# Channel mixing of the last layer moved from in front of the key scans to between and behind them

## What is computed

```python
x = x + _L3_attn_ref(xn, ...) + _L3_ffn_ref(xn, L3_ffn_W_r, L3_ffn_W_k, L3_ffn_W_v, L3_ffn_mu_r, L3_ffn_mu_k)

# attention: dx is a convolution over three tokens, less x
t5 = jnp.tanh((x + dx * maa_x) @ maa_w1).reshape(B, T, 5, 32)
m = jnp.einsum('btfc,fcd->fbtd', t5, maa_w2)
xw = x + dx * (maa_w + m[0])                     # also xk, xv, xr, xg
w_log = -jnp.exp(time_decay + jnp.tanh(xw @ decay_w1) @ decay_w2)
S = jnp.exp(wt)[..., None] * S + kt[..., None] * vt[..., None, :]     # forwards, and likewise backwards
yn = ((yg - mu) / jnp.sqrt(var + eps)).reshape(B, T, D) * ln_w + ln_b
return yn * g @ Wo                               # y is also gated by sigmoid(dx @ gate_w + gate_b)

# channel mixing
xr = mu_r * x + (1.0 - mu_r) * x_prev
xk = mu_k * x + (1.0 - mu_k) * x_prev
out = sigmoid(xr @ W_r.T) * (square(relu(xk @ W_k.T)) @ W_v.T)
```

## Time and profile before

| | |
|---|---|
| median of 3 runs | 2244.57 us |
| the profiled execution's own time | 2241.96 us |
| its span | 2240.1 us |
| last layer behind its layernorm | from about 1940 us to the end |
| TensorE matmul busy, whole span | 1997.6 us (89%) |
| VectorE busy, whole span | 1578.4 us (70%) |

### The profile page before, as it was taken

One profiled execution on the slowest core, in us unless ns is written; L12 is line 12 of the kernel. 1 busy time (PEld: TensorE's weight loads), 2 busy tenths in 40 slices (PEclk: granted clock), 3 DMA queues, 4 the chain that ended last, 5 costly groups with the idle time before them and its releaser, 6 DMA issues. The chain is left out here.

```text
span 2240.1 us, 56828 instructions
## 1 busy us (share of the span) xinstructions
PE 1997.6 (89%) x22888; PEld 1359.7 (61%) x22888; DVE 1578.4 (70%) x4071; ACT 1300.6 (58%) x2606; POOL 978.3 (44%) x1206
## 2 busy tenths in 40 slices
PE   4669998998999999999999797789999998688886
PEld 2548887996888887888888675533333343333322
DVE  6666664675666677767666645489898993689996
ACT  3337775555777777777777533147776777444323
POOL 2027776664667844566443224011111210058763
PEclk9779999999999999999999889679999999799998
DMA  7221111314011200000000017211111110000000
GB/s 186 97 78 37 39 38 48 100 30 159 21 38 20 39 7 2 21 2 21 2 2 3 1 53 233 63 23 39 39 39 39 40 41 4 27 0 1 10 5 24
DMA packets 77797, 93.46 MB, mean 42 GB/s; under 512 B 10017, under 2 KB 56114, under 8 KB 76002
## 3 DMA queue, kind: packets, MB, share of 16 engines
q1 hardware_dynamic: 64050, 76.54, 11.4%
q0 software_dynamic: 13488, 13.28, 3.0%
HBM read 53.87 MB, written 35.53 MB: 40 GB/s over the span
## 5 line engine op out<-in xcount | busy, mean ns | idle before, releaser
L1181 DVE TENSOR_REDUCE a_parts<-a_S 128x1 f32<-128x512 f32 (+1 forms) x576 | 362.8, 682 | 30.5 <-PE a_S L1065 24.3
L1152 ACT ACTIVATE WA<-a_E 128x1024 f32<-128x1024 f32 (+1 forms) x320 | 282.9, 939 | 119.0 <-PE a_E L1093 60.8
L478 POOL TENSOR_SCALAR WA<-WA,a1b_rinv 128x1024 f32<-128x1024 f32 (+3 forms) x192 | 142.0, 757 | 181.4 <-DVE a1b_rinv L817 181.2
L1057 PE MATMUL a_S<-a_KS,a_QS 54*128 54x512 bf16 (+3 forms) x768 | 190.1, 348 | 30.8 <-DVE a_parts L1181 18.8
L478 POOL TENSOR_SCALAR XR<-XR,a1b_rinv 128x768 f32<-128x768 f32 (+3 forms) x192 | 141.2, 749 | 118.4 <-DVE a1b_rinv L817 117.7
L633 PE MATMUL a1b_O<-a1b_PT,WA 128*64 128x128 f32 x3072 | 189.0, 276 | 0.0
L633 PEld LDWEIGHTS a1b_O<-a1b_PT,WA 128*64 128x64 f32 x3072 | 165.8, 137 | 6.5
L1057 PEld LDWEIGHTS a_S<-a_KS,a_QS 54*128 54x128 bf16 x768 | 58.8, 95 | 173.6 <-DVE a_parts L1181 136.2
L598 PE MATMUL a1b_B<-a1b_Kf,a1b_Qf 64*128 64x512 f32 (+2 forms) x768 | 155.1, 478 | 8.5 <-issue 4.6
L993 POOL CAST a_mrow<-WA 32x128 bf16<-32x128 f32 x16 | 4.5, 280 | 355.2 <-DVE WA L1194 355.2
L1105 PE MATMUL a_O<-WA,V 128*9 128x512 f32 (+3 forms) x1536 | 154.5, 489 | 0.1
(11 more groups left out here) (551 smaller groups left out, 5786.5 us busy)
## 6 DMA issues: line engine op xcount, KB each, us to landing
WA<-in_w SPq DMA_DIRECT2D x7, 1024.0 KB, 9.5
a_QS<-qstack SPq DMA_DIRECT2D x32, 216.0 KB
a_KS<-kstack SPq DMA_DIRECT2D x32, 216.0 KB
a1b_tb<-tab SPq DMA_DIRECT2D x12, 512.0 KB
qstack<-f_parts SPq DMA_DIRECT2D x24, 256.0 KB
kstack<-f_parts SPq DMA_DIRECT2D x24, 256.0 KB
f_slots<-f1r_zrows SPq DMA_DIRECT2D x9, 516.0 KB
f1t_xs<-f_slots SPq DMA_DIRECT2D x9, 516.0 KB, 7.3
```

What stands on the lines that cost most here:

```text
L478: pool.tensor_scalar(v, v, rinv[:, e, u, part:part + 1], 1.0, ALU.mult, ALU.mult).then_inc(n_sb, 1)
L1057: ins = pe.matmul(pS[(at + half) % SB][:, lo:lo + n], QS[s][ROW[half], pair, i * P:(i + 1) * P], KS[s][ROW[half], pair, block * P:block * ...
L1152: act.activation(PT[q % NP][:, :, 0:w], pE[q % 2][:, :, 0:w], ACT.Exp).then_inc(e_sb, 1)
L1181: dve.tensor_reduce(peak, pS[at % SB][:, :].rearrange("p (c k) -> p c k", c=n), AX.X, ALU.max)\
```

## The change

No chunk of the channel mixing lies in front of the first scan any more. Six lie between the scans: chunk 0 in steps 4 to 6 of batch 1, chunk 1 in the same steps of batch 2, and chunks 2 to 5 in batch 3, one for each two steps. Chunks 6 and 7 lie behind. The interpolation is gone: GpSimd makes four scaled weight matrices once, at the end of batch 0 (`weights`), and the products c_k and c_r are two accumulated matmuls each, on the tokens and on the tokens one earlier. The middle chunks' products c_k, c_r, c_v, c_t go through the ring of the two pC banks; ScalarE's part of them is `middle`, VectorE's parts are `weighed_mid` and `collect_mid`.

In front of the first scan t5b, d1 and d2 of batch 0 go to pY ("FRONT") and pass the ring by; m_g of batch 0 and its mixing move behind the first scan; the products k come after `values(0)`; and GpSimd no longer waits for the interpolation. In step 7 the output product of the batch before now lies between r and g. At the end the normalisation of batch 3 is done in halves by two VectorE operations each, `scaled` and `final`, without ScalarE's affine step, and one-element activations on ScalarE load the tables of tanh and, at the end, of the logarithm early. ScalarE calls `middle(c)` behind `deviation` or `decay` in batches 1 and 2, and between the steps of the normalisation in batch 3.

```diff
...
-    EARLY = 3
-    SLOT = tuple(c % 3 for c in range(2 * B))
-    LAST_IN = (None, None, None) + tuple(range(2 * B - 3))
-    mdx, mxr, mxk = (ph.sb(n, [P, 3, CH]) for n in ("mdx", "mxr", "mxk"))
-    mkr = [Sf[0][:, 0:CH], Sf[0][:, CH:T], Sf[1][:, 0:CH]]
-    mdelta = [Sr[0][:, 0:CH], Sr[0][:, CH:T], Sr[1][:, 0:CH]]
-    msig = [Sf[1][:, CH:T], Sr[1][:, CH:T], Sr[2][:, 0:CH]]
-    low = [t[:, 0:CH] for t in (*pV, pY)]
-    high = [t[:, CH:T] for t in (*pV, pY)]
-    l_dx, l_mixed, l_rk, l_relu, l_k2, l_sig, l_v, l_delta, l_tr, l_x = (
-        ph.sem(n) for n in ("ldx", "lmixed", "lrk", "lrelu", "lk2", "lsig", "lv", "ldelta", "ltr", "lx"))
+    MID = (0, 1, 2, 3, 4, 5)
+    SLOT = {6: 0, 7: 1}
+    TURN = {c: n for n, c in enumerate(SLOT)}
+    ck, cr, cw = (ph.sb(n, [P, T]) for n in ("ck", "cr", "cw"))
+    mkr = [Sf[0][:, 0:CH], Sf[0][:, CH:T]]
+    mdelta = [Sr[0][:, 0:CH], Sr[0][:, CH:T]]
+    msig = [Sr[1][:, 0:CH], Sr[1][:, CH:T]]
+    low = [t[:, 0:CH] for t in pV]
+    high = [t[:, CH:T] for t in pV]
+    FRONT = {("t5b", 0, 0): pY[:, CH:T], ("d1", 0, 0): pY[:, 0:CH], ("d2", 0, 0): pY[:, 0:CH], ("d2", 0, 1): pY[:, CH:T]}
+    sides = (slice(0, CH), slice(CH, T))
...
-    START = {0: NEXT[0], 1: NEXT[1], 2: NEXT[2], 3: NEXT[3][:1], 4: NEXT[4], 5: NEXT[3][1:], 6: NEXT[5][3:],
-             7: NEXT[5][2:3] + NEXT[6]}
+    STILL = {0: ((("r", 0),), (("r", 1),), (("m_g", 0), ("m_g", 1))), 2: ((("gate", 0),), (("gate", 1),)),
+             3: ((("g", 0),), (("g", 1),))}
+    START = (("t5a", 0),), (("t5a", 1),), (("t5b", 0),), (("m_w", 0), ("m_v", 0)), (("m_w", 1), ("m_v", 1)), (("d1", 0),), \
+        (("m_k", 0), ("m_r", 0)), (("d2", 0), ("d2", 1)), (("m_k", 1), ("m_r", 1)), (("k", 0),), (("k", 1),)
+    ONE = {4: (("c_k", 0), ("c_r", 0)), 5: (("c_v", 0),), 6: (("c_t", 0),)}
+    FOUR = {0: (("c_k", 2), ("c_r", 2)), 1: (("c_v", 2),), 2: (("c_t", 2), ("c_k", 3), ("c_r", 3)), 3: (("c_v", 3),),
+            4: (("c_t", 3), ("c_k", 4), ("c_r", 4)), 5: (("c_v", 4),), 6: (("c_t", 4), ("c_k", 5), ("c_r", 5)), 7: (("c_t", 5),)}
...
-        after = of(b + 1, NEXT[v]) if b + 1 < B else []
         front = of(b - 1, LAST.get(v, ())) if b else of(0, STILL.get(v, ()))
-        return after + front if v == 7 else front + after
-
-    ring = [key for v in range(HK) for group in of(0, START[v]) for key in group]
+        if b + 1 == B:
+            return ([(("c_v", 5, 0),)] if v == 7 else []) + front + [((kind, c, 0),) for kind, c in FOUR[v]]
+        after = of(b + 1, NEXT[v])
+        mixing = [((kind, b - 1, 0),) for kind, c in ONE.get(v, ())] if b else []
+        return (after[:2] + front + after[2:] if v == 7 else front + after) + mixing
...
+        key = (kind, b, h)
+        return FRONT[key] if key in FRONT else pC[turn_of[key] % 2]
...
+            def weights():
+                pool.tensor_scalar(wk1[:, :], mw_k, mu_k, None, ALU.mult)
+                pool.tensor_scalar(wr1[:, :], mw_r, mu_r, None, ALU.mult).then_inc(l_wd, 1)
+                pool.wait_ge(l_wd, 1)
+                pool.tensor_tensor(wk0[:, :], mw_k, wk1[:, :], ALU.subtract)
+                pool.tensor_tensor(wr0[:, :], mw_r, wr1[:, :], ALU.subtract).then_inc(l_w, 1)
...
-            pool.wait_ge(l_mixed, EARLY)
...
-                n = place[kind, b, h]
+                if (kind, b, h) in FRONT:
+                    if kind == "d2":
+                        pe.wait_ge(emptied["t5b"], 1)
+                    return
+                n = turn_of[kind, b, h]
...
+                elif kind == "c_k":
+                    pe.wait_ge(l_w, 1)
+                    pe.matmul(out[:, :], wk1[:, :], tokens(b, 1), start=True, stop=False)
+                    ins = pe.matmul(out[:, :], wk0[:, :], tokens(b, 0), start=False, stop=True)
+                elif kind == "c_r":
+                    pe.matmul(out[:, :], wr1[:, :], tokens(b, 1), start=True, stop=False)
+                    ins = pe.matmul(out[:, :], wr0[:, :], tokens(b, 0), start=False, stop=True)
+                elif kind == "c_v":
+                    pe.wait_ge(m_k2, MID.index(b) + 1)
+                    ins = pe.matmul(out[:, :], mw_v, ck[:, sides[MID.index(b) % 2]], start=True, stop=True)
+                elif kind == "c_t":
+                    pe.wait_ge(emptied["c_v"], MID.index(b) + 1)
+                    lo = MID.index(b) % 2 * CH
+                    for t in range(CT):
+                        ins = pe.transpose(out[:, t * P:(t + 1) * P], cw[:, lo + t * P:lo + (t + 1) * P], G["ident"][:, :])
...
+            step(of(0, START[:9]))
+            values(0)
+            step(of(0, START[9:]))
...
+                    else:
+                        first_k(6)
+                        first_r(6)
...
-            first(3)
-            first(4)
+            second(6)
+            turn(6)
+            first_k(7)
             add(NS - 2)
-            second(3)
+            first_r(7)
             product("cen", B - 1, 0)
             product("cen", B - 1, 1)
-            second(4)
-            turn(3)
-            first(5)
+            second(7)
             product("var", B - 1, 0)
             product("var", B - 1, 1)
-            first(6)
-            turn(4)
-            second(5)
-            first(7)
-            second(6)
-            turn(5)
+            turn(7)
             product("out", B - 1, 0)
             product("out", B - 1, 1)
-            turn(6)
-            second(7)
-            turn(7)
...
+                for cut in cuts:
+                    act.activation(rs[:, cut], rs[:, cut], ACT.Exp, scale=-0.5).then_inc(rs_sb, 1)
...
+            def middle(c):
+                m = MID.index(c)
+                act.wait_ge(c_ps, place["c_k", c, 0] + 1)
+                act.activation(ck[:, sides[m % 2]], bank("c_k", c, 0)[:, :], ACT.Relu).then_inc(emptied["c_k"], 1)
+                act.wait_ge(emptied["c_k"], m + 1)
+                act.activation(ck[:, sides[m % 2]], ck[:, sides[m % 2]], ACT.Square).then_inc(m_k2, 1)
+                act.wait_ge(c_ps, place["c_r", c, 0] + 1)
+                act.activation(cr[:, sides[m % 2]], bank("c_r", c, 0)[:, :], ACT.Sigmoid).then_inc(emptied["c_r"], 1)
...
             act.wait_ge(consts, 3)
             begin(0)
+            act.activation(warm[:, :], eps[:, :], ACT.Tanh)
             evacuate("t5a", 0)
             evacuate("t5b", 0)
-            chunk(0)
-            scale_x(1, 0)
-            chunk(1)
-            scale_x(1, 1)
+            begin(1)
             evacuate("d1", 0)
-            chunk(2)
...
+            chunk(6)
+            chunk(7)
             evacuate("cen", B - 1)
             squares(B - 1)
-            chunk(5)
+            act.activation(warm[:, :], eps[:, :], ACT.Ln)
             evacuate("var", B - 1)
             deviation(B - 1)
-            chunk(6)
-            shape(B - 1)
-            chunk(7)
...
+            def scaled(h):
+                cut = cuts[h]
+                dve.wait_ge(rs_sb, 2 * B - 1 + h)
+                dve.scalar_tensor_tensor(yc[:, cut], yc[:, cut], w["ln_w"], rs[:, cut], ALU.mult, ALU.mult).then_inc(last_sb, 1)
+
+            def final(h):
+                cut = cuts[h]
+                dve.wait_ge(last_sb, h + 1)
+                dve.wait_ge(emptied["g"], 2 * B)
+                dve.scalar_tensor_tensor(yg[:, cut], yc[:, cut], w["ln_b"], g[(B - 1) % 2][:, cut], ALU.add,
+                                         ALU.mult).then_inc(gn_sb, 1)
...
+            def weighed_mid(c):
+                m = MID.index(c)
+                dve.wait_ge(c_ps, place["c_v", c, 0] + 1)
+                dve.wait_ge(emptied["c_r"], m + 1)
+                dve.tensor_tensor(cw[:, sides[m % 2]], cr[:, sides[m % 2]], bank("c_v", c, 0)[:, :],
+                                  ALU.mult).then_inc(emptied["c_v"], 1)
+
+            def collect_mid(c):
+                rows = X[:, c * CT:(c + 1) * CT, :]
+                if c:
+                    dve.wait_ge(emptied["out"], {1: 2, 5: 6}.get(c, 4))
+                dve.wait_ge(c_ps, place["c_t", c, 0] + 1)
+                dve.tensor_tensor(rows, rows, bank("c_t", c, 0)[:, :].rearrange("p (k d) -> p k d", k=CT),
+                                  ALU.add).then_inc(emptied["c_t"], 1)
+                dve.wait_ge(emptied["c_t"], MID.index(c) + 1)
+                dve.sem_inc(l_x, 1)
...
             begin(0)
-            interpolate(0)
-            interpolate(1)
-            interpolate(2)
             mix("w", 0, 0)
             mix("v", 0, 0)
-            weighed(0)
             mix("w", 0, 1)
             mix("v", 0, 1)
-            weighed(1)
-            collect(0)
             add_x(0, 0)
             add_x(0, 1)
             mix("k", 0, 0)
             mix("r", 0, 0)
-            collect(1)
-            weighed(2)
             mix("k", 0, 1)
             mix("r", 0, 1)
-            mix("g", 0, 0)
-            mix("g", 0, 1)
-            collect(2)
...
+                    if n == 0:
+                        mix("g", 0, 0)
+                        mix("g", 0, 1)
```

(68 more changed lines are left out.)

121 lines of the change are left out of this document (42 added, 79 removed).

## The result

The changed kernel takes **2254.03 us** (median of 14 runs, 2248.35 to 2262.62); the kernel before takes 2246.19 us (14 runs, 2243.22 to 2250.49). The ratio is 1.0036, 95% interval 1.0025 to 1.0048: slower by 8 us. The forecast was 2245.2 us, +0.6, in a range from 2236 to 2252: the sign fits, the time lies above the range.

A forecast was written before the change was run, and what follows sets the result against it. TensorE's chain was taken to bound the front, nearly full TensorE and VectorE batches 1 and 2, VectorE alone batch 3. Terms -13.1 + 2.1 + 10.8 - 5.2 + 6.0 = +0.6 on 2244.57 gave 2245.2 us, range 2236 to 2252.

The forecast's parts named there:

- term 5: TensorE's clock: four falls on the path, one each in batches 1 and 2, two in batch 3; +6.0 us.
- Term 3: Batches 1 and 2: c_k waits for its bank, delaying the sum and second m_k; +5.4 us each, 10.8 in all.
- Term 4: Batch 3 and the end: added VectorE work and waits +7.6, shorter end -12.7; taken as -5.2 us.
- Term 1: In front of the first scan: interpolation and matmuls of `first` and `second` go; first step earlier, -13.1 us.
- the first scan starts later than 1967: Sign that the prediction is wrong; the first scan step was expected at about 1964.6 in place of 1977.75.
- Term 2: Batch 0: g mixings move between its first two steps, putting TensorE's queue later; +2.1 us.
- The slow rival: TensorE falls to half clock at most new waits; all eight candidates give +6.6, 2251.2 us; chance 0.25.

The follow-up runs named there:

- after2: The changed kernel, unedited, run and traced a second time; ratio to the kernel before 1.0036.
- late2: Changed kernel with chunks 0 and 1's c_k, c_r moved behind the sum and values, c_t and `collect_mid` behind the output product or operation; ratio to before 0.9988.
- fill: Changed kernel with 13 unread dense matmuls put between the small products in front of the first scan; ratio to the kernel before 1.0060.
- fill2: Changed kernel with only four unread dense matmuls between the small products in front of the first scan; ratio to the kernel before 1.0031.
- fill2b: The run fill2 again, on the same chip as after2; ratio to the kernel before 1.0031.

## Why the prediction was wrong

The mechanisms named were the right ones; sizes failed. The forecast was 8.8 us too low: 7.2 in the difference (+0.6 for +7.8) and 1.6 in the reference.

The step that failed most is **term 5**, the price of TensorE's lower clock: four falls of 1.5 us, +6.0, "between 0 and 9". On the path it was 9.6 us in after2 (5.0 in batches 1 and 2, 4.6 in batch 3 and the end) and 12.7 in the first trace (6.3 in front, 6.4 in batches 1 and 2), both above the upper bound. Terms 3 and 4 were short by 1.5 and 1.7. Term 1 came out nearly right in one trace; in the four others the front gained 4 to 7 us less than said, again with the clock down.

By the second trace of the changed kernel, whose layer is longer by as much as the medians differ (308.0 - 300.0 = +8.0), term by term:

- **Term 1** said -13.1 and measured 25.2 - 37.7 = -12.5, with the full clock. The first trace gave -6.1, and all five average 29.2 us, -8.5. The forecast named one gap here, "1.4 in front of the second m_w", and put no fall on the path: taking nine dense matmuls and three groups of transposes out of the front left a stretch of small products in which the clock fell in four of five traces. What they had cost was counted; what their going did to the clock was not. The sign "the first scan starts later than 1967" came in the first trace (1971.6 on the scale of the kernel before), not in after2 (1965.3).
- **Term 2** said +2.1 and measured +2.0, in every trace with that front but late2 and fill (3.2 and 3.3, with a slow t5a product in each).
- **Term 3** said 64.6 us and 1.5 for one fall, 66.1 in each batch. Batch 1 took 67.0 in both traces. In after2 the wait for the second m_k product is 6.62 us (said: 1.23 + 5.2) and the transposes start 55.0 us into the batch (said: 2087.0 - 2032.05 = 55.0); the sum behind them ran slow. VectorE and TensorE of after2:

```profile
2067.16 0.75 DVE L2651 SCALAR_TENSOR_TENSOR a_xk<-a_C,WA 128x512 f32<-128x512 f32 x1 [6.62 <-PE a_C L2383]
```
```profile
2076.23 0.66 PE L2352 MATMUL a_C<-ident,a_cw 128*128 128x128 f32 x4 [1.85 <-DVE a_xg L2651]
2076.81 3.58 PE L2413 MATMUL a_Y<-a_Sr,WA 128*32 128x512 f32 x8
```
  Batch 2 took 68.6, with two falls. In the first trace it took 70.0, since there one fall slowed all four matmuls of c_k and c_r, 3.1 us for one fall (the first of them here):

```profile
2136.46 2.08 PE L2340 MATMUL a_C<-XNT,a_wk 128*128 128x512 f32 x2 [2.76 <-DVE a_xk L2651]
```
  Without their falls the two batches come to 135.6 - 5.0 = 130.6, not 129.2, which is +12.3 and not +10.8: a size.
- **Term 4** said -5.2. In the first trace, where no product of batch 3 ran slow, batch 3 and end take 86.2 us for 89.7 before, -3.5: the end was 31.3 for 30.3 and the steps 54.9 for 54.3. Mis-sized by 1.7 against the -5.2.
- **Term 5** said four falls of 1.5, 6.0. After2 has five on the path, one in batch 1, two each in batches 2 and 3: 1.7, 1.7, 1.6, 1.7 and 2.9 us, 9.6 in all. The last is dearer because three groups of matmuls ran slow behind one gap (TensorE of after2):

```profile
2207.49 2.07 PE L2343 MATMUL a_C<-XNT,a_wr 128*128 128x512 f32 x2 [3.20 <-DVE X L2709]
2209.36 1.92 PE L2344 MATMUL a_C<-XNT,a_wr 128*128 128x512 f32 x2
2211.20 2.94 PE L2413 MATMUL a_Y<-a_Sr,WA 128*32 128x512 f32 x8
```
  The terms so measured, -12.5 + 2.0 + 12.3 - 3.5 + 9.6, make +7.9. In the first trace -12.5 + 2.0 + 12.3 - 3.5 + 12.7 make +11.0, for 11.1. The slow rival, which had a chance of 0.25, named this mechanism and this place, with all eight candidates at 1.5; five dearer ones and the misses of terms 3 and 4 were enough.
- **What stays open**: the execution of after2 took 2249.58 us, 4.9 under the median of its eight runs, as the profiled one of the kernel before, 2241.96, lies 4.2 under the median of 14. That the two fit the medians' difference is in part luck: with the mean front of the five traces the sum would be 4 us higher. Which falls make up the median is not shown.
- **The reference**: 1.6 us more come from the median of three runs, 2244.57, to which I added; over 14 runs it is 2246.19.

Gaps on TensorE cost more than their length in the front too, where I had reckoned none on the path. The Trainium skill ("TensorE: Matmul & The Clock Gate", section "Why this matters for your kernels") wants matmuls to stay back-to-back, but what it warns of are idle gaps longer than these; the forecast gave the rule without that condition. Fill, fill2 and fill2b agree with the first: with the gaps filled the clock stayed up. That shorter gaps are harmless fits after2, where gaps of 1.54 and 0.81 us cost nothing more, and not the four traces in which the clock fell behind such gaps.

For the table of the exponential the rows of both kernels' ends (before, then changed) show no drain behind the load; the activation ahead of the changed kernel's load ended at 2247.60, so there is none in front of it either. The Trainium skill ("ScalarE: Activation LUTs", section "What ACT_TABLE_LOAD costs") has one of about 1.38 us at each switch; these traces do not agree:

```profile
2221.35 1.28 ACT L2515 ACT_TABLE_LOAD   x1
2222.64 1.06 ACT L2515 ACTIVATE a_rs<-a_rs 128x1024 f32<-128x1024 f32 x1
...
2247.62 1.28 ACT L2531 ACT_TABLE_LOAD   x1
2248.91 1.15 ACT L2531 ACTIVATE a_rs<-a_rs 128x512 f32<-128x512 f32 x2
```
